# The scan of the context rows moved from TensorE to GpSimd and accumulating transfers

## The reference

```
h   = rmsnorm(layernorm(x)) * g_res @ W_in.T + b_in
u   = exp(-0.001) * (rmsnorm(ctx) * g_init)[:, 0:512]
s_t = a * s_(t-1) + u_t                 over the 512 rows, a = exp(-dt), about 0.001
x2  = x + h + s[plug]                   plug: the patch that each row belongs to, from the patch lengths
y   = layernorm(x2)
xr, xk = mixes of each row of y with the row before it (mu_r, mu_k)
out = x2 + sigmoid(xr @ W_r.T) * (relu(xk @ W_k.T)^2 @ W_v.T)
```

## Time and profile before

| | |
|---|---|
| median of 3 runs | 786.76 us (786.43 to 787.09) |
| profiled execution, its own time | 788.05 us |
| its span | 786.5 us, 11081 instructions |
| TensorE matmul / weight load busy | 756.9 / 624.1 us |
| VectorE busy | 553.8 us |
| ScalarE busy | 413.3 us |
| GpSimd busy | 173.4 us |
| indirect transfers of GpSimd (L426) | 60 and 4, mean 1656 and 2012 ns of GpSimd each |
| DMA | 85.73 MB, mean 109 GB/s |

### The profile page before, as it was taken

The page is one execution under the profiler, slowest core; times in us unless marked ns, Lnnn a source line. Parts: engine busy times, 40 slices in busy tenths (PEclk is TensorE's granted clock), DMA queues, the critical chain, the costliest instruction groups (busy, mean ns, idle before and its releaser), DMA issues.

```text
span 786.5 us, 11081 instructions
## 1 busy us (share of the span) xinstructions
PE 756.9 (96%) x3462; PEld 624.1 (79%) x3463; DVE 553.8 (70%) x1005; ACT 413.3 (53%) x681; POOL 173.4 (22%) x175
## 2 busy tenths in 40 slices
PE   7669899999999999999999999999999999999997
PEld 4457688888888888888888888888888888888876
DVE  4678797685866868586686858667685867667452
ACT  3317755454654645466464546656454665544760
POOL 7244131311213131121313112131311213130000
PEclk9879999999999999999999999999999999999999
DMA  7476153441706244170624417062441706231011
GB/s 256 150 188 166 60 124 132 112 143 47 209 2 167 88 110 144 46 208 0 156 98 109 144 43 211 0 166 88 108 146 41 212 0 160 94 102 20 1 54 54
DMA packets 42765, 85.73 MB, mean 109 GB/s; under 512 B 3536, under 2 KB 3536, under 8 KB 42704
## 3 DMA queue, kind: packets, MB, share of 16 engines
q1 hardware_dynamic: 30624, 63.71, 21.7%
q0 software_dynamic: 9216, 16.78, 13.5%
q10 hardware_dynamic: 2880, 4.76, 1.7%
HBM read 64.26 MB, written 21.76 MB: 109 GB/s over the span
## 4 chain that ended last, share of the span: by engine, by line
PE 85%; DVE 4%; POOL 4%; issue 2%; ACT 2%; DMA 1%; DVEq 0%; POOLq 0%; ACTq 0%
PE bank L484 27%; PE bank L486 27%; PE bank L485 27%; PE bank L588 3%; POOL ring L426 2%; DMA s_rows<-scanned 1%; POOL decay L363 1%; DVE xk_lo L894 1%; DVE scratch L989 0%; DVE ring L1019 0%; DVE gate L1044 0%; ACT scratch L794 0%; POOL rs_a L389 0%; DVE bn_a L923 0%; DVE bn_b L1025 0%
## 5 line engine op out<-in xcount | busy, mean ns | idle before, releaser
L426 POOL DMA_INDIRECT ring<-s_rows,patch_now x60 | 99.4, 1656 | 245.8 <-DMA s_rows<-scanned 214.6
L894 DVE TENSOR_TENSOR xr_lo<-scratch,xr_hi 128x512 fp32r<-128x512 f32 x124 | 85.6, 690 | 68.9 <-ACT xr_hi L704 68.4
L989 DVE SCALAR_TENSOR_TENSOR scratch<-turned,cols,scratch 128x512 f32<-128x512 f32 x128 | 94.6, 749 | 34.4 <-ACT scratch L749 15.0
L484 PE MATMUL bank<-wi_hi,xt_hi 128*128 128x512 f32 x256 | 104.0, 406 | 5.1 <-DVE xt_lo L894 5.1
L704 ACT ACTIVATE turned<-bank 128x512 f32<-128x512 f32 x64 | 33.4, 604 | 143.3 <-PE bank L588 114.7
L484 PE MATMUL bank<-xk_hi,wk_hi 128*128 128x512 f32 x256 | 99.9, 390 | 2.2 <-DVE xk_lo L894 2.2
L485 PE MATMUL bank<-wi_lo,xt_hi 128*128 128x512 f32 x256 | 101.8, 398 | 0.0
L486 PE MATMUL bank<-wi_hi,xt_lo 128*128 128x512 f32 x256 | 101.5, 396 | 0.0
L484 PE MATMUL bank<-wr_hi,xr_hi 128*128 128x512 f32 x256 | 99.7, 389 | 0.8 <-DVE xr_lo L894 0.8
L486 PE MATMUL bank<-xk_hi,wk_lo 128*128 128x512 f32 x256 | 99.6, 389 | 0.0
L485 PE MATMUL bank<-xk_lo,wk_hi 128*128 128x512 f32 x256 | 99.6, 389 | 0.0
(11 more groups left out here) (131 smaller groups left out, 1283.5 us busy)
## 6 DMA issues: line engine op xcount, KB each, us to landing
ring<-in_x SPq DMA_DIRECT2D x16, 1024.0 KB, 7.4
out<-gate SPq DMA_DIRECT2D x64, 256.0 KB
xt<-in_x_turned SPq DMA_DIRECT2D x15, 1024.0 KB, 5.2
ctx_rows<-in_ctx SPq DMA_DIRECT2D x16, 512.0 KB, 8.0
s_rows<-scanned ACTq DMA_DIRECT2D x16, 256.0 KB, 2.0
gate<-in_L_xattn_W_in SPq DMA_DIRECT2D x4, 256.0 KB, 3.4
xt<-in_x_turned SPq DMA_DIRECT2D x2, 512.0 KB, 6.3
turned<-in_L_ffn_W_r SPq DMA_DIRECT2D x1, 1024.0 KB, 7.8
```

Source lines behind the costliest of these rows:

```text
L426: pool.indirect_dma_start(ring[b.slot][:, t, :], None, s_rows[:, :], bass.IndirectOffsetOnAxis(ap=rows, axis=0), compute_op=ALU.add).then_ ...
L484: nc.tensor.matmul(where, lhs_hi, rhs_hi, start=start, stop=False)
L894: return nc.vector.tensor_tensor(to, whole, high, ALU.subtract)
L989: nc.vector.scalar_tensor_tensor(scratch[:, 2 + i % 2, :], turned[:, c, 1:S + 1], cols[:, 1 + which, c:c + 1], scratch[:, i % 2, :], ALU.m ...
```

## The change

From the third batch on (new = 2 and later) TensorE's scan, u_hi, u_lo and scan_out are left out. GpSimd makes the scan in four steps instead. With k = 8, 4, 2, 1 it writes `weakened` = a^k * u, waits for that, and issues a transfer that adds rows 0 to 127-k of `weakened` to rows k to 127 of u; each step waits for the transfer of the one before. After the four, u holds the sum over 16 earlier rows with their powers (a^13 and later count as 0). Then GpSimd adds the bias and writes `scanned`. The store and the patches stay as they are.

scan_input of new moves on VectorE from behind the third ka_low to right behind norm_b. SP's loads for new now come as ctx, x, x turned; ctx waits for the far branch of the batch before as well. The far branch computes its first tile (rows 0 to 127) again to have the hi and lo parts of u, since they are not made any more.

```diff
+def shift_steps(powers):
+    return [(k, powers[k] if k < len(powers) else 0.0) for k in (8, 4, 2, 1)]
...
 (sp, iteration)
+                    reached(sp, far_over, new.plus(-1), 1, 1)
                     rows_added(sp, new.plus(-1))
-                    reached(sp, xt_lo_ready, new.plus(-1), 2, 2)
-                    load_xt(new)
+                    load_ctx(new)
                     reached(sp, out_ready, b.plus(-1), T, T)
...
                     load_x(new)
-                    reached(sp, far_over, new.plus(-1), 1, 1)
-                    load_ctx(new)
+                    reached(sp, xt_lo_ready, new.plus(-1), 2, 2)
+                    load_xt(new)
...
 (gpsimd)
+            def shift_scan(b):
+                since = b.plus(-2)
+                for n, (k, power) in enumerate(steps_of_scan):
+                    if n == 0:
+                        reached(pool, u_ready, b, 1, 1)
+                    reached(pool, later_added, since, 16 * STEPS, 16 * n)
+                    hold(pool, pool_passed)
+                    nc.gpsimd.tensor_scalar(weakened[:, :], u[:, :], power, None, ALU.mult).then_inc(weakened_ready, 1)
+                    reached(pool, weakened_ready, since, STEPS, n + 1)
+                    hold(pool, pool_passed)
+                    pool.dma_start(u[k:P, :], weakened[0:P - k, :], accum_op=ALU.add).then_inc(later_added, 16)
+
+            def add_bias(b):
+                reached(pool, later_added, b.plus(-2), 16 * STEPS, 16 * STEPS)
+                reached(pool, s_stored, b, 16, 0)
+                nc.gpsimd.tensor_tensor(scanned[:, :], u[:, :], bias[:, :], ALU.add).then_inc(s_copied, 1)
...
                 if new.exists(B):
+                    if not is_first(new, 1):
+                        shift_scan(new)
+                        add_bias(new)
                     far(new)
                     add_patches(new)
...
 (tensor)
                 if new.exists(B):
-                    scan(new)
                     far(new)
...
 (scalar)
                 elif new.exists(B):
-                    if not is_first(b):
-                        u_high(new)
                     store_scan(new)
...
 (vector)
                 if nxt.exists(B):
                     norm_b(nxt)
+                if new.exists(B):
+                    scan_input(new)
                 for m in range(C):
                     if b.exists(B):
                         ka_low(b, m)
                     if new.exists(B):
                         if m in (1, 2):
                             x_lo(new, m - 1)
-                        if m == 2:
-                            scan_input(new)
...
-                if new.exists(B):
-                    u_low(new)
...
                 if new.exists(B):
-                    scan_out(new)
                     far(new)
```

More of the change, by code:

```diff
@@ L96, in build @@
     powers = decay_powers()
+    steps_of_scan = shift_steps(powers)
+    STEPS = len(steps_of_scan)
+    assert len(powers) <= 2 ** STEPS
     input_gain = math.exp(-EPSILON)
@@ L162, in build @@
         patch_now = sb("patch_now", [P, T], U32)
+        weakened = sb("weakened", [P, D])
         def part(row, start, shape, dt):
@@ L213, in build @@
             "u_ready u_hi_ready u_lo_ready s_done s_copied s_stored patch_picked")
+        weakened_ready, later_added = sems("weakened_ready later_added")
         dep_added = [sem(f"dep_added{t}") for t in range(T)]
@@ L405, in far @@
                 with pool.If(n[0] > 0):
[L406 to L410, removed]
+                    for c in range(T):
+                        tiles, done = n[1] * T + c + 1, n[1] * (T - 1) + c
+                        if c == 0:
+                            reached(pool, s_copied, b, 1, 1)
                         else:
-                            pool.wait_ge(far_u, done - 1)
+                            pool.wait_ge(far_u, tiles - 1)
                         hold(pool, pool_passed)
                         pool.dma_start(ctx_rows[:, :], ctx[b.number(), c * P:(c + 1) * P, :]).then_inc(far_loaded, 16)
-                        pool.wait_ge(far_v, done)
+                        pool.wait_ge(far_v, tiles)
                         nc.gpsimd.tensor_tensor(rs_c[:, :], v_c[:, 1:2], half[:, 0:1], ALU.pow).then_inc(far_rs, 1)
+                        if c == 0:
+                            continue
                         pool.wait_ge(far_copied, done)
@@ L519, in far @@
                             pe.wait_ge(far_copied, done - 1)
-                        else:
-                            reached(pe, s_copied, b, 1, 1)
+                        pe.wait_ge(far_u_lo, n[1] * T + c)
                         product(scan_bank(b)[:, :], decay_hi[:, 1, :], decay_lo[:, 1, :], u_hi[:, :], u_lo[:, :],
                                 True, False).then_inc(far_carried, 1)
-                        pe.wait_ge(far_u_lo, done)
+                        pe.wait_ge(far_u_lo, n[1] * T + c + 1)
                         product(scan_bank(b)[:, :], decay_hi[:, 0, :], decay_lo[:, 0, :], u_hi[:, :], u_lo[:, :],
@@ L584, in turn @@
                     if t == SCAN and b.plus(1).exists(B) and not is_first(b):
-                        reached(pe, s_copied, b.plus(1), 1, 1)
                         reached(pe, far_over, b.plus(1), 1, 1)
@@ L945, in scan_input @@
                 reached(dve, rs_c_done, b, 1, 1)
-                reached(dve, u_lo_ready, b.plus(-1), 1, 1)
+                if b.fixed and b.number() < 3:
+                    reached(dve, u_lo_ready, b.plus(-1), 1, 1)
+                else:
+                    reached(dve, s_copied, b.plus(-1), 1, 1)
                 nc.vector.scalar_tensor_tensor(u[:, :], ctx_rows[:, 0:D], rs_c[:, :], g_ctx[:, :],
@@ L953, in far @@
                 with dve.If(n[0] > 0):
-                    for c in range(1, T):
-                        done = n[1] * (T - 1) + c
-                        dve.wait_ge(far_loaded, done * 16)
+                    for c in range(T):
+                        tiles, done = n[1] * T + c + 1, n[1] * (T - 1) + c
+                        dve.wait_ge(far_loaded, tiles * 16)
                         for h in range(2):
                             nc.vector.bn_stats(bn_c[:, 6 * h:6 * h + 6], ctx_rows[:, h * D:(h + 1) * D]).then_inc(far_bn, 1)
-                        dve.wait_ge(far_bn, done * 2)
+                        dve.wait_ge(far_bn, tiles * 2)
                         hold(dve, dve_passed)
                         nc.vector.bn_aggr(mv_c[:, :], bn_c[:, :]).then_inc(far_mv, 1)
-                        dve.wait_ge(far_mv, done)
+                        dve.wait_ge(far_mv, tiles)
                         nc.vector.scalar_tensor_tensor(v_c[:, 0:1], mv_c[:, 0:1], mv_c[:, 0:1], mv_c[:, 1:2],
                                                        ALU.mult, ALU.add).then_inc(far_ms, 1)
-                        dve.wait_ge(far_ms, done)
+                        dve.wait_ge(far_ms, tiles)
                         nc.vector.tensor_scalar(v_c[:, 1:2], v_c[:, 0:1], RMS_EPS, None, ALU.add).then_inc(far_v, 1)
-                        dve.wait_ge(far_rs, done)
+                        dve.wait_ge(far_rs, tiles)
                         nc.vector.scalar_tensor_tensor(u[:, :], ctx_rows[:, 0:D], rs_c[:, :], g_ctx[:, :],
                                                        ALU.mult, ALU.mult).then_inc(far_u, 1)
-                        dve.wait_ge(far_u, done)
-                        dve.wait_ge(far_carried, done)
+                        dve.wait_ge(far_u, tiles)
+                        if c > 0:
+                            dve.wait_ge(far_carried, done)
                         nc.vector.tensor_copy(u_hi[:, :], u[:, :]).then_inc(far_u_hi, 1)
-                        dve.wait_ge(far_u_hi, done)
+                        dve.wait_ge(far_u_hi, tiles)
                         low(u_lo[:, :], u[:, :], f32(u_hi[:, :])).then_inc(far_u_lo, 1)
+                        if c == 0:
+                            continue
                         dve.wait_ge(far_s, done)
```

## The result

The changed kernel takes 962.03 us (median of 4 runs, 960.52 to 963.13); the kernel before, on the same chip, 786.6. The ratio is 1.223 (95% interval 1.2209 to 1.2251). The forecast was 825 us with a range from 780 to 905: the sign was right, the size far off, and the time lies outside the range.

The account below looks back on a forecast made before the run. TensorE, busy 96%, was taken as the limit; GpSimd's chain ahead of ScalarE's turn copy would lengthen 13 periods by 31 us and the first by 7, so 788.05 + 38 = 826, 825 by the median; range 780 to 905.

Parts of the forecast that it names:

- The sum: Whole kernel: period 48.35 us, 2.4 longer, times 13 is 31; first turn copy 7 us late; +38 us, to 826.
- The chain, L = 20.5 us: GpSimd's four scan steps of 4.8 us each and a bias addition of 1.3; ends 13.0 and 34 us.
- the landing: Issue to landing of each accumulating GpSimd transfer: 3.5 us, between 2.0 and 5.8; called the step most likely off.
- The top of the range, 905: Upper end with the chain exposed: steps of 6.2 us (median indirect transfer), or 5.3 with late loads.
- xt, put at 23.6: Load of turned x, now last: lands about 23.6 us after the turn copy, against its use at 24; hidden.
- The clock, 0: TensorE's granted clock: 0.99 where busy 51.56 of 56 us, so nothing was charged for its waits.
- The hop of 27.4 us: From ScalarE's turn copy to u ready on VectorE: mean of 26.85 twice and 28.4 once.
- part 3: SP's loads in the new order: x and turned x land hidden by less than half a us; cost 0.
- The first chain: First of 14 batches: u ready at 90.42, store out at 111.35, turn copy 7.65 us late, less 0.7.
- Few DMA engines: Rival on the scan's transfers: odd row counts fall on few engines, 26 us more a batch, 1189 us; chance 0.19.

Follow-up runs that it names:

- pe_kept_busy: The changed kernel (four steps) with 38 matmuls of unused result added behind TensorE's turn, to fill its wait; 942.88 us, ratio 1.1999.
- old_loads: The changed kernel with SP's old order of loads (x turned, x, ctx); 962.49 us, ratio 1.2233.
- two_steps: The changed kernel with only the scan steps of 2 and 1 rows; 787.22 us, ratio 1.0007 to the kernel before.
- plain_transfers: The changed kernel with its 56 scan transfers writing instead of adding, so the scan's sum is left out; 889.96 us, ratio 1.1307.

## Why the prediction was wrong

The mechanism stood: the scan's matmuls are worth 0.68 us a batch, and the chain, ahead of ScalarE's turn copy, costs what it is longer than its room. The failure is in two terms of the sum: above all the length of the chain, put at 20.5 us and measured at 27.6, and then the fall of the clock, put at nothing and measured at about 20 us in all.

**The sum.** In the profiled execution 136 us were missing (962 against 826). A period is 57.83 us where the prediction had 48.35: the chain is 7.1 longer, the hop from the turn copy to u 2.2 (29.6), the store and its wake 0.2. Times 13 that is 123. The first turn copy is at 121.22 instead of 111.35, another 10. This makes 133 of the 136; the last 3 stay open.

**The chain, L = 20.5 us.** This is the step that failed most. In the batch shown it is 27.3 (441.49 to 468.79), and in the mean 27.6; 7.1 x 14 = 99 of the 136 us are its own. Lines of all 56, by GpSimd's group, by the tile's view, and the landings:
```profile
L445 POOL TENSOR_SCALAR weakened<-u 128x512 f32<-128x512 f32 x56 | 90.9, 1624 | 163.2 <-DMA u<-weakened 139.8 <-DVE u L981 23.3
```
```profile
L445 POOL TENSOR_SCALAR weakened<-u x56: 1483/1496/2176, 94.3 to 865.1; 128x512 f32<-128x512 f32 x56
...
DMA to landing us min/median/max: 3.7/4.0/5.0
```

| piece of a step | predicted, us | measured | off in four steps |
|---|---|---|---|
| scaling | 0.75 | 1.62 mean (1.5; the second of a batch 2.1) | 3.5 |
| own write and gap to the issue | 0.46 | 0.62 | 0.6 |
| issue to landing | 3.5 | 4.0 | 2.0 |
| landing to the next instruction | 0.1 | 0.2 | 0.4 |
| u to the first scaling (once) | 0 | 0.3 | 0.3 |
| bias addition (once) | 1.3 | 1.26 | 0 |

The table adds up to the 6.8 of the batch shown; the mean is 0.3 longer, as four landings take 4.7 to 5.0 and one issue comes 2 us late. The largest miss is the scaling; the prediction held the landing to be most likely off. I took a value near the memsets, though the operation reads, computes and writes; the row of the same kind was the affine_select, and four times its 371 ns are 1.48, the upper end in the prediction and what was measured. With that end and the quickest accumulating transfer of the trace, 4.3, the chain would have been 26.7 us by the same sum. I had argued from the nearest rows and then twice picked a value below them.

**The top of the range, 905.** It was said to be steps of 6.2 us, with the median indirect transfer. By the prediction's own pieces a step with that landing of 5.8 is 0.75 + 0.16 + 0.30 + 5.8 + 0.1 = 7.1, the chain 29.7 and the time 954; its upper end for the chain, 34, would give 1014. So the range was cut below its own bounds, and with them it would have held the 962. A smaller slip is xt, put at 23.6: 2.5 MB at the rate used for x give 24.5, half a us behind its use. It cost next to nothing: in the changed kernel ScalarE waits for xt once, for 1.5 us.

**The clock, 0.** I charged nothing because the clock was 0.99 in a stretch of 92% busy. That row averaged short waits. One wait of 9.4 us in each batch is another thing: from 471.0 to 527.9 TensorE is busy 47.23 of 56.90 us and its clock is 0.92. `pe_kept_busy` prices it at 20 us or somewhat more. It lies on the loop, as projection and gate product stand between the turn copy and the square of ctx.

**The hop of 27.4 us** from the turn copy to u was 29.6 in the mean: the clock (1.6) and 0.6 us more, together 29 us over 13 periods. In `pe_kept_busy` 7 of the 13 hops are 27.1 to 27.4, as the prediction has it, so the path itself was right. x lands late, as part 3 feared (1.4 us of wait, 12 times), but `old_loads` shows that its order is not what decides. How the 0.6 divides between x and GpSimd's roots is not settled; it is worth 8 us.

**The first chain.** I had it begin at 90.4, right behind u. root_a stands ahead of it in iteration 0 and waits for the statistics of x, so it began at 94.3, though u was ready at 88.4. The prediction went through the order on ScalarE and not, for this one iteration, through that on GpSimd. Of the 10 us at the first turn copy 7 are the chain's length and 3 this late start; in two_steps it cost 7, and it alone kept that kernel from its gain.

**Few DMA engines** is refuted, as the one-row transfer alone would have taken over 20 us: the four transfers of a batch, of 120, 124, 126 and 127 rows, land after 4.2, 3.7, 4.0 and 4.0 us. The Trainium skill (DMA: Bandwidth & Descriptors, Why a DMA increments its semaphore by 16) states the rule of this rival with an exception for some direct copies issued by GpSimd; the accumulating ones from tile to tile behave here as by the exception. The Trainium skill's fit for a transfer issued by GpSimd (same page, Anatomy of one DMA) gives, as an estimate, 2.6 us: the plain ones took 2.9, the accumulating ones 4.0.

## What to carry to other kernels

When work moves to a chain of dependent small operations, its length decides, not its busy time: write down the room between the last input and the first instruction queued behind the result, and take for each link the nearest row of the same kind (reads, writes, both), not a value below it. Each link pays its waits too: here 0.8 us of 6.4 is neither work nor transfer. Drop links that carry nothing: two of the four steps were below float32's reach. Without them, and with the first root out of the way, the idea gains 7 us where it had lost 175.

## What the runs showed of the hardware

- GpSimd scales 128x512 float32 in 1.5 us and adds two such tiles in 1.26; VectorE's additions of that size took 0.69. That the scaling, with one input, is the slower of the two was unexpected.
- A scaling that begins inside one of VectorE's two-input operations takes longer. The second scaling of the batch shown, 448.33 to 450.45, begins 0.8 us before the end of this subtraction and takes 2.1 us:
```profile
447.88 1.22 DVE L924 TENSOR_TENSOR xt_lo<-xt,xt_hi 128x1024 fp32r<-128x1024 f32 x1
```
In the traces of the eight kernels with steps, 102 scalings begin over 0.15 us before the end of such an operation. 95 end 1.35 us (within 0.03) behind it, whatever is left of it, up to 1.2 us. The other 7 stand against `gate<-bank,gate`, which has one input in a TensorE bank, and take 1.5 us. In plain_transfers most second scalings begin ahead of the subtraction and take 1.5 as well. No run moved VectorE's operations by themselves.
- A transfer from tile to tile issued by GpSimd lands 2.9 us after its issue, an accumulating one 4.0, whether of 120 or of 127 rows.
- After a wait of 9.4 us TensorE's clock is at 1.2 GHz for the first 6 to 14 matmuls of the projection, 0.43 us each instead of 0.23.
